# Sixteen-element attention chain: bias or mask and the extremum of each head in one VectorE instruction

## The reference

```python
sim = jnp.einsum('bhnd,bhmd->bhnm', q, k)
sim = (sim + rel_pos_bias(rel_emb, n, m)) * SCALE
attn = jax.nn.softmax(sim, axis=-1)
```

## Time and profile before

| | |
|---|---|
| median of 3 runs | 1412.81 us (1411.97 to 1413.31) |
| the profiled execution | 1414.21 us |
| its span, first to last instruction | 1411.0 us |
| instructions | 25836 |
| TensorE busy (matmuls) | 1261.4 us |
| VectorE busy | 959.5 us |
| ScalarE busy | 783.4 us |
| GpSimd busy | 339.1 us |
| mean granted clock of TensorE | 0.956 |

### The profile page before, as it was taken

How to read it: one execution, slowest core, us unless ns; L and a number is a source line. 1 busy time by engine, 2 the same in 40 slices (tenths; PEclk the granted TensorE clock), 3 DMA queues, 4 the chain that set the end, 5 groups by cost and what they waited for, 6 DMA issues and landing times.

```text
span 1411.0 us, 25836 instructions
## 1 busy us (share of the span) xinstructions
PE 1261.4 (89%) x9426; PEld 996.6 (71%) x9426; DVE 959.5 (68%) x1877; ACT 783.4 (56%) x2690; POOL 339.1 (24%) x766
## 2 busy tenths in 40 slices
PE   3567889999999999999999999999999999988755
PEld 2345667877787887877787778788787778766633
DVE  2355466969687877868696968777786869583522
ACT  1124364857565666757475756566675847464411
POOL 0101313231322232232323132223223232302020
PEclk9779999999999999999999999999999999999755
DMA  6901010100001010101000000101010100000000
GB/s 200 331 1 41 1 42 1 34 16 19 29 0 48 0 48 0 45 4 45 4 25 23 15 33 0 48 0 48 0 45 4 45 4 11 27 5 4 4 4 4
DMA packets 28586, 44.38 MB, mean 31 GB/s; under 512 B 4710, under 2 KB 20614, under 8 KB 28044
## 3 DMA queue, kind: packets, MB, share of 16 engines
q1 hardware_dynamic: 26252, 31.41, 7.0%
q0 software_dynamic: 2304, 12.58, 2.5%
HBM read 37.65 MB, written 6.34 MB: 31 GB/s over the span
## 4 chain that ended last, share of the span: by engine, by line
PE 64%; DVE 21%; ACT 11%; issue 2%; DMA 1%; POOL 1%; SPq 0%; POOLq 0%; DVEq 0%; ACTq 0%
PE psum L487 43%; PE psum L481 7%; ACT A L790 5%; ACT sa_p L790 4%; DVE small_ L1003 4%; PE psum L642 3%; PE psum L535 3%; PE psum L694 2%; PE psum L706 2%; PE psum L661 2%; DVE A L997 2%; DVE sa_p L1011 1%; DVE sa_p L997 1%; PE psum L551 1%; DVE A L1088 1%
## 5 line engine op out<-in xcount | busy, mean ns | idle before, releaser
L1279 POOL TENSOR_SCALAR small_<-small_ 128x1 f32<-128x1 f32 x112 | 37.1, 331 | 865.3 <-ACT A L908 382.5
L790 ACT ACTIVATE A<-A,small_ 128x128 f32<-128x128 f32 x384 | 148.6, 393 | 86.0 <-DVE small_ L1004 86.0
L481 PE MATMUL psum<-cst,A 128*128 128x128 f32 x672 | 108.3, 288 | 64.4 <-DVE A L1011 27.0
L783 ACT ACTIVATE A<-psum 128x1024 f32<-128x1024 f32 (+2 forms) x112 | 77.1, 688 | 156.9 <-PE psum L481 109.1
L481 PEld LDWEIGHTS psum<-cst,A 128*128 128x128 f32 x672 | 80.3, 147 | 101.4 <-DVE A L1011 40.5
L1168 DVE SCALAR_TENSOR_TENSOR A<-psum,half_cw,A 128x127 f32<-128x127 f32 (+2 forms) x288 | 75.2, 343 | 41.1 <-ACT A L894 41.1
L790 ACT ACTIVATE sa_p<-sa_p,small_ 128x128 f32<-128x128 f32 x256 | 99.1, 397 | 4.4 <-DVE small_ L1004 4.4
L790 ACT ACTIVATE ca_p<-ca_p,small_ 128x128 f32<-128x128 f32 x256 | 98.7, 391 | 4.8 <-DVE small_ L1004 4.8
L1010 DVE RECIPROCAL small_<-small_ 128x8 f32<-128x8 f32 x112 | 22.3, 199 | 91.1 <-ACT A L790 81.5
L997 DVE TENSOR_TENSOR A<-psum,cst 128x1024 f32<-128x1024 f32 x32 | 39.2, 1225 | 56.9 <-PE psum L535 56.9
L790 ACT ACTIVATION_READ_ACCUMULATOR A<-A,small_ 128x1 f32 x384 | 73.8, 192 | 0.0
(11 more groups left out here) (217 smaller groups left out, 3213.6 us busy)
## 6 DMA issues: line engine op xcount, KB each, us to landing
inT<-in_tokT SPq DMA_DIRECT2D x16, 256.0 KB, 2.9
kv_rows<-A SPq DMA_DIRECT2D x16, 256.0 KB
ctx_in<-in_ctx SPq DMA_DIRECT2D x16, 128.0 KB, 2.1
A<-bias_rows SPq DMA_DIRECT2D x1, 2048.0 KB, 9.3
Wsakv<-in_wsa_kv SPq DMA_DIRECT2D x1, 2048.0 KB, 12.7
Wcakv<-in_wca_kv SPq DMA_DIRECT2D x1, 2048.0 KB, 14.0
ctx_end<-in_tokT SPq DMA_DIRECT2D x16, 128.0 KB, 2.2
out<-x_out SPq DMA_DIRECT2D x16, 128.0 KB, 1.7
```

The costliest lines, as they stand in the source:

```text
L481: mm = pe.transpose(out[:, c * P:(c + 1) * P], src[:, c * P:(c + 1) * P], ident)
L783: return act.activation(out, in_, ACT.Copy)
L790: ins = act.activation(p[:, h * T:(h + 1) * T], p[:, h * T:(h + 1) * T], ACT.Exp, bias=sm(part, "nm", w * HU + h, w * HU + h + 1), accum_o ...
L1279: then(pool.tensor_scalar(t, src, scale, eps, ALU.mult, ALU.add))
```

## The change

All softmaxes work on negated scores. The scaling of the queries (l0, sa, ca, c3), the bias table, the window mask and the padding mask change their sign. `softmax_max` becomes `softmax_low`: for each head one VectorE instruction adds the bias or mask to 128 columns of scores, writes the sum to SBUF and writes the minimum of the head to its column of `nm`. That minimum of the negated scores is the negated maximum which the exponential needs as its bias, so the separate maximum and negation are gone, and the exponential takes the scale -1. One semaphore per layer, `lows`, is raised after the fourth and after the eighth head. ScalarE's exponentials wait for it half a unit at a time. TensorE's second group of scores in sa and ca waits for the eighth head of the first unit, where it waited for the add. The VectorE engine no longer waits for itself inside the step; one semaphore increment (`held`) stands ahead of the eight instructions. In the diff below the four lines in which the engines receive the new helper are left out.

```diff
@@ -23,6 +23,7 @@
 NEG = -1.0e9
+TOP = 3.0e38
 LOG_A_CAP = 80.0
@@ -72,7 +73,7 @@
     put("upto", (p <= j) * 1.0)
-    put("window", np.where((j >= p - 64) & (j < p + 65), 0.0, NEG))
+    put("window", np.where((j >= p - 64) & (j < p + 65), 0.0, -NEG))
     put("quad", (p // HD0 % 4 == np.arange(4)) * 1.0)
@@ -161,8 +162,7 @@

-NAMES += [f"{L}_{step}" for L in ("l0", "sa", "ca", "c3") for step in ("scores", "negmax", "exp", "probs", "PT", "PTsb")]
-NAMES += ["sa_added", "ca_added"]
+NAMES += [f"{L}_{step}" for L in ("l0", "sa", "ca", "c3") for step in ("scores", "lows", "exp", "probs", "PT", "PTsb")]

@@ -290,7 +290,7 @@

-        _soft = [("mx", 2 * HU), ("nm", 2 * HU), ("sm", 2 * HU), ("rc", 2 * HU)]
+        _soft = [("nm", 2 * HU), ("sm", 2 * HU), ("rc", 2 * HU)]
         _norm = [("bn", 6), ("mv", 2), ("r", 1), ("r1", 1), ("ssq", 1), ("ssq1", 1), ("t1", 2)]
@@ -376,7 +376,11 @@

-            return need, free, need_unit
+            def need_lows(t, L, w, half):
+
+                eng.wait_ge(sem[f"{L}_lows"], t.value(2, half + 1) if L == "c3" else t.value(4, 2 * w + half + 1))
+
+            return need, free, need_unit, need_lows

@@ -633,7 +637,7 @@
                         if w == 1:
-                            need_unit(t, f"{L}_added", 0)
+                            need_lows(t, L, 0, 1)
                         else:
@@ -785,9 +789,10 @@
                 part = PART[L]
-                need_unit(t, f"{L}_negmax", w)
                 for h in range(HU):
-                    ins = act.activation(p[:, h * T:(h + 1) * T], p[:, h * T:(h + 1) * T], ACT.Exp,
+                    if h % (HU // 2) == 0:
+                        need_lows(t, L, w, h // (HU // 2))
+                    ins = act.activation(p[:, h * T:(h + 1) * T], p[:, h * T:(h + 1) * T], ACT.Exp, scale=-1.0,
                                          bias=sm(part, "nm", w * HU + h, w * HU + h + 1),
@@ -973,7 +978,7 @@
             then(dve.tensor_copy(keep[:], pad_at))
-            dve.tensor_scalar(pad_add[:], keep[:], NEG, None, ALU.mult)
+            dve.tensor_scalar(pad_add[:], keep[:], -NEG, None, ALU.mult)
             then(dve.tensor_scalar(keep[:], keep[:], -1.0, 1.0, ALU.mult, ALU.add))
@@ -981,7 +986,7 @@
                 dve.wait_ge(sem["bias_ps"], 1)
-                dve.tensor_scalar(rows_at, Pd[0:2 * H2, 0:2 * T - 1], HD2 ** -0.5, None, ALU.mult).then_inc(sem["bias_sb"], 1)
+                dve.tensor_scalar(rows_at, Pd[0:2 * H2, 0:2 * T - 1], -HD2 ** -0.5, None, ALU.mult).then_inc(sem["bias_sb"], 1)

@@ -990,18 +995,21 @@

-            def softmax_max(t, L, w, p, scores, extra):
-
-                mx, nm = (sm(PART[L], name, w * HU, (w + 1) * HU) for name in ("mx", "nm"))
+            def held():
+
+                dve.sem_inc(sem["dve_chain"], 1)
+                steps[0] += 1
+
+            def softmax_low(t, L, w, p, scores, extra):
+
                 need_unit(t, f"{L}_scores", w)
-                ins = dve.tensor_tensor(heads(p), heads(scores), extra, ALU.add)
-                if L in LAYER:
-                    ins.then_inc(sem[f"{L}_added"], 1)
-                    need_unit(t, f"{L}_added", w)
-                else:
-                    then(ins)
-                then(dve.tensor_reduce(mx, heads(p), AX.X, ALU.max))
-                dve.tensor_scalar(nm, mx, -1.0, None, ALU.mult).then_inc(sem[f"{L}_negmax"], 1)
+                held()
+                for h in range(HU):
+                    at = slice(h * T, (h + 1) * T)
+                    ins = dve.tensor_tensor_reduce(p[:, at], scores[:, at], extra(h), 1.0, TOP, ALU.add, ALU.min,
+                                                   sm(PART[L], "nm", w * HU + h, w * HU + h + 1))
+                    if h % (HU // 2) == HU // 2 - 1:
+                        ins.then_inc(sem[f"{L}_lows"], 1)

@@ -1037,7 +1045,7 @@
                     ins = dve.tensor_scalar(q0o[:, c * T:(c + 1) * T], Pa[:, c * T:(c + 1) * T], pc("bq", c),
-                                            HD0 ** -0.5, ALU.add, ALU.mult)
+                                            -HD0 ** -0.5, ALU.add, ALU.mult)
                 ins.then_inc(sem["q0_sb"], 1)
@@ -1122,7 +1130,7 @@
                         at = slice(w * BANK, (w + 1) * BANK)
-                        dve.tensor_scalar(Q2[L][:, at], X[:, at], HD2 ** -0.5, None, ALU.mult).then_inc(sem[f"{L}_q_sb"], 1)
+                        dve.tensor_scalar(Q2[L][:, at], X[:, at], -HD2 ** -0.5, None, ALU.mult).then_inc(sem[f"{L}_q_sb"], 1)

@@ -1135,7 +1143,7 @@
                 return {f"{L}_hat": [hats], f"{L}_q": [queries],
-                        **{f"{L}_s{w}": [lambda t, w=w: softmax_max(t, L, w, (PA2, PB2)[w][L][:], X, heads(bias[:, LAYER[L], w]))]
+                        **{f"{L}_s{w}": [lambda t, w=w: softmax_low(t, L, w, (PA2, PB2)[w][L][:], X, lambda h: bias[:, LAYER[L], w, h * T:(h + 1) * T])]
                            for w in range(2)},
@@ -1213,7 +1221,7 @@
                 need(t, "c3_q")
-                dve.tensor_scalar(q3, Pd[:, 0:D], float(np.float32(1.0 / np.sqrt(HD3))), None,
+                dve.tensor_scalar(q3, Pd[:, 0:D], -float(np.float32(1.0 / np.sqrt(HD3))), None,
                                   ALU.mult).then_inc(sem["c3_q_sb"], 1)
@@ -1224,7 +1232,7 @@
                 "inputs": [inputs], "kv0": [project0],
-                **{f"l0_s{w}": [lambda t, w=w: softmax_max(t, "l0", w, probs0, P_1, spread(C("window"), HU))] for w in range(2)},
+                **{f"l0_s{w}": [lambda t, w=w: softmax_low(t, "l0", w, probs0, P_1, lambda h: C("window"))] for w in range(2)},
                 **{f"l0_p{w}": [lambda t, w=w: softmax_norm(t, "l0", w, probs0)] for w in range(2)},
@@ -1232,7 +1240,7 @@
                 "m_xh": [m_mix], "m_heads": [m_gated], "m_out": [result_m], "kv3": [keys_values3], "hat3": [normed3],
-                "q3": [query3], "c3_s": [lambda t: softmax_max(t, "c3", 0, probs3, P_4, spread(pad_add[:], HU))],
+                "q3": [query3], "c3_s": [lambda t: softmax_low(t, "c3", 0, probs3, P_4, lambda h: pad_add[:])],
                 "c3_p": [lambda t: softmax_norm(t, "c3", 0, probs3)], "c3_out": [result3],
```

More of the change, by code:

```diff
@@ L475, in _ @@
             pe.sem_inc(sem["c3_kv"], 1)
-            need, free, need_unit = need_by(pe)
+            need, free, need_unit, need_lows = need_by(pe)
             def turn(out, src, n):
@@ L779, in _ @@
             act.wait_ge(sem["prep_done"], 2)
-            need, free, need_unit = need_by(act)
+            need, free, need_unit, need_lows = need_by(act)
             def copy(out, in_):
@@ L940, in _ @@
             steps = [0]
-            need, free, need_unit = need_by(dve)
+            need, free, need_unit, need_lows = need_by(dve)
             def step(ins):
@@ L1251, in _ @@
             steps = [0]
-            need_names, free, need_unit = need_by(pool)
+            need_names, free, need_unit, need_lows = need_by(pool)
             def restart():
```

## The result

The changed kernel takes 1391.42 us (median of 4 runs, 1385.49 to 1395.54) against 1412.39 for the kernel before beside it: a ratio of 0.985, 95% interval 0.981 to 0.989, so 21 us faster. The forecast was 1397 with 1390 to 1422. Two further timings in the experiments agree: 0.985 (0.983 to 0.988) and 0.984 (0.982 to 0.987). The profiled execution took 1390.1 with a span of 1388.2; before it was 1414.21 and 1411.0. The two are not equally typical: 1390.1 is in the middle of the changed kernel's 15 timings, while 1414.21 is 3.1 above the median of the 42 timings of the kernel before (1411.1; two of them are slower). Differences between these two traces, the opening's above all, hold for the pair and are larger than those of the medians.

The account below looks back on a forecast made before the run. TensorE was taken to bound the loop, chains of waits the opening and end. Loop 5.2, opening 5.6 and end 5.8 make 16.6 us off the median 1412.81: 1396.2, named 1397, range 1390 to 1422.

Parts of the forecast that it names:

- The number: Whole kernel: 16.6 us saved from the median 1412.81 gives 1396.2, named as 1397.
- What bounds the kernel: TensorE is busy 75.06 of 76.52 us per loop turn, only 1.46 winnable; chains of waits decide opening and end.
- The price of the new instruction: VectorE, per head: 0.20 pass plus 0.09 read, x = 0.29 us; a unit takes 2.35 against 2.59.
- the tiny VectorE row: A tiny VectorE operation occupying 0.08 us, the neighbour from which the accumulator read was priced at 0.09.
- Earlier exponentials: ScalarE starts after four heads, 1.21 us after the unit's start against 2.72, so 1.5 sooner.
- bare units: Softmax units in opening and end with add, exponentials and product all on the chain; each wins 1.5 us.
- The wait that is added: TensorE's second score group waits for all eight instructions, 2.35 us against 1.22; in the loop hidden by 0.45.
- Inside the loop: Per turn 0.27 before the second sa probabilities' turn and 0.13 of small pieces: 0.40 x 13 = 5.2 us.
- Opening: 0 to 200 us: three units at 1.5, one at 0.7, VectorE time of two 0.4: 5.6 us won.
- nothing takes this back: Opening: its gain stays, as the weights have landed and POOL's folding at 141 starts when its input comes.
- End: From 1192 us: two c3_s units 3.0, steps around 1264 to 1275 1.8, the rest 0.7 and 0.27: 5.8 us.
- The rival of a VectorE bound: Loop: past x = 0.325 four units outgrow VectorE's 0.15 slack; 1423 at 0.36, 1445 at 0.40; chance 0.24.

Follow-up runs that it names:

- full_wait: The changed kernel, but ScalarE's exponentials of a unit wait for all eight heads: 1398.05 us, ratio 0.9915; timed again 1395.77 us, ratio 0.9891.
- rows_first_before: The kernel before, with the second element's inputs and the store of rows issued ahead of the late weights: 1416.76 us, ratio 1.0041.
- rows_alone_before: The kernel before, second element's inputs and first row store ahead of the late weights, which SyncE holds until the first gather lands: 1408.07 us, ratio 0.998.
- fused_plus_plain: The changed kernel, with four plain adds of 128 columns ahead of each four fused instructions: 1483.0 us, ratio 1.0521 to the kernel before.
- halves_old_ops: The kernel before, its add, maximum and negation done in halves of four heads, exponentials starting behind each half: 1433.65 us, ratio 1.0158.
- eight_adds: The kernel before, its one add of 1024 columns made as eight of 128, all else as it was: 1447.36 us, ratio 1.0254.

## Why the prediction was right, step by step

- **The number**: 15.8 us were forecast from the median and 21.0 measured. The first median, 1391.42, lies 1.4 inside the range, and the third, 1388.93, outside it. The mechanisms of loop and end held; the opening's gain came in good part for reasons that the forecast did not have, and that part is luck.
- **What bounds the kernel**: right. The loop gave little per turn, opening and end gave two thirds of the pair's 22.8.
- **The price of the new instruction**: the step with the largest error. The forecast priced a head at x = 0.29, the pass at 0.20 and the read at 0.09. Measured: 0.211, of which a plain pass is 0.197. The lower bound of 0.20 (the read costs nothing) was nearly the truth; the tiny VectorE row that I took as a model for the read was the wrong neighbour, because the read is hidden beside the next head's pass. A unit takes 1.69, not 2.35. The Trainium skill's table in "VectorE: DVE Perf Modes" ("The TRN2 errata") gave an estimate of 2.55 a unit; the trace disagrees, 1.69. The Trainium skill's rule there ("Two Vector instructions with no wait between them") that such an operation is two instructions agrees with the trace, which has 896 read records; that the second one costs the 58 cycles I had put into that estimate from the table's other column does not.
- **Earlier exponentials**: 1.5 sooner forecast; 0.97 instead of 2.72 after the unit's start, so 1.75 sooner. The bare units' waits shrank by 1.59 (7.57 to 5.98, 7.50 to 5.91), 1.61 and 1.60. The 0.16 between goes with the added semaphore increment: the end's chain has 0.19 from the product's end (1372.93) to the first fused instruction, with L1000 in it, where it was 0.02 (1394.19 to 1394.21). I had put 0.03; no run takes the increment out alone. Full_wait splits the 1.59: 0.84 is the early start, 0.75 the shorter unit and what it loses to the increment.
- **The wait that is added**: free in the loop, as predicted (no idle of TensorE before ca_s1). In the last element it shows: 1.04 before ca_s1 (1288.73), where 0.34 stood for the add, 0.7 that I had not counted. TensorE's next wait gives it back: 1.50 where 2.95 stood, so both together are 0.75 shorter.
- **Inside the loop**: 0.40 a turn forecast, 0.57 or 0.58 measured. The 0.27 before the sa probabilities went, as said, but not because of the half-unit start: full_wait has the same turn. The shorter unit alone does it. Comparing the two turns place by place, the changed one is up to 0.9 ahead at the turn of the c3 probabilities, and 0.3 of that is given back at the near-key chain ([0.54] to [0.86]): a chain that starts from TensorE's own query product, and that does not get shorter. That was predicted to stay; it grew by what reached it early.
- **Opening**: 5.6 forecast, 8.2 measured, and yet the step "nothing takes this back" was wrong, and so was its reason, "the weights have landed by then": SyncE still issues weights until 56.3. The first element's lead of 6.8 us went down to 0.3 at a store and its gather, and with it the 3.2 of the two bare units that the forecast counted on (3.0); the rest of that lead was clock. What came behind it: 1.6 of wait in the third bare unit and 0.4 in the next small waits; 1.7 because the eight products behind that unit ran at the full clock (5.40 at 103.98, 3.70 at 101.81); 2.5 where POOL folds Wmi and Wmo, shown below; and 1.4 from there to the loop's entry, 0.8 of it from the third element's l0 (forecast 0.7); the remaining 0.3 are small pieces. So two errors of opposite sign stand in this term: 3.0 of the forecast never reached the second element, and 4.2 came from TensorE's clock level, which the forecast did not contain. The 1.7 is not shown to belong to the change: the eight products took 3.70 in rows_first_before too, behind the same old wait of 2.72, and 5.40 in rows_alone_before.
- **End**: 5.8 forecast; 7.3 less the thirteenth turn's 0.6 is 6.7. By unit: the two bare c3_s waits of 3.85 and 7.50 became 2.26 and 5.91 (3.2, forecast 3.0); the three waits of 0.53, 1.20 and 0.86 became none, 0.55 and 0.33 (1.7, forecast 1.8). Of the three units with VectorE alone on the chain (forecast 0.24 each) sa_s0 gave 0.53 (TensorE's wait of 1.29 became 0.76) and the first ca unit the 0.75 above; for the third no such wait stands out. Some 0.5 is left; products of the end run at the lower clock in either kernel, not at the same places, which I did not separate.
- **The rival of a VectorE bound** did not come true, since x stayed far under 0.34. Its place is shown: units of 3.03 cost 23 and 37 us, and TensorE waits where the rival said. The slope is about 4.8 a turn for each us of unit (4.51 less the mean 2.1 of the two others, over 0.5), where I had 4; carried back from there it reaches the turn before at a unit of about 2.6 (3.03 less 2.1 / 4.8), near the 2.63 of the forecast (8 x 0.325 and the 0.03), an estimate that no run stands at. The forecast would have missed badly had the read cost what ScalarE's does (0.40 a pair).

The place of the 2.5 us, TensorE's timeline of the kernel before and of the changed one around the turn that waits for POOL's folding (POOL L1320, L1328; 7.08 and about 3.6 for its two parts in both):

```profile
153.96 0.69 PE L481 MATMUL psum<-cst,sa_p 128*128 128x128 f32 x2 [5.21 <-DVE sa_p L1019]
154.44 6.14 PE L487 MATMUL psum<-Wcakv,ca_p 128*128 128x512 f32 x8
```

```profile
142.75 5.01 PE L491 MATMUL psum<-ca_p,Wcakv 128*128 128x128 f32 x32
...
149.90 0.44 PE L485 MATMUL psum<-cst,sa_p 128*128 128x128 f32 x2 [1.08 <-DVE sa_p L1027]
150.18 3.60 PE L491 MATMUL psum<-Wcakv,ca_p 128*128 128x512 f32 x8
```

The turn is 4.06 earlier in the changed kernel, as the chain through VectorE and POOL that it waits for. Its shorter idle time is no gain: the products ahead of it ran slower (5.01 for 32, 3.74 before). But behind it the eight products take 3.60 instead of 6.14. The granted clock is 1.00 and then 0.66 in the kernel before (10 us from 140 and from 150 on), and 0.73 and then 1.00 in the changed one: the low stretch lies ahead of the wait in the one, where the wait hides it, and behind it in the other. In the thirteen profiled executions the four that idled 2.4 or more at this turn (the kernel before, its two reorderings and fused_plus_plain) took 6.14, 4.87, 4.96 and 4.80 for these eight, and the nine that idled about 1.0 took 3.60. Among the nine are halves_old_ops and eight_adds, with the old instructions and dearer units, so the 2.5 is not the price of the old softmax either. Whether the long idle time lowers the clock, or a low stretch that comes earlier merely shortens the idle time, no run separates.

Not settled: why TensorE's clock level in the opening differs between executions of one kernel (full_wait), and how much of the change's median rests on it. No experiment held the opening's clock fixed, and there is one trace of the unaltered kernel before, a slow one.

## What to carry to other kernels

Price a fused instruction by its start-to-start step in a run of its own kind, and give both bounds for its second record: here the read was free and the new unit cost a third less than the three instructions it replaced, although it has sixteen records for three. Starting the consumer at half a unit pays only where the unit is bare (0.84 each here); where the engine is 98% busy the shorter unit is the gain. And when a prologue gets faster, look at what it now arrives beside: a store or gather that found free DMA queues may meet the weight loads, and moving it ahead of them helped here only when the loads also waited until the gather had landed. Before dividing a gain of some 20 us between stretches of two traces, see how far executions of one kernel differ there: here by 6 us.

## What the runs showed of the hardware that was not expected

- A VectorE accumulator read (82 ns) starts together with the next instruction and adds no step: fused with read 0.211 a head, plain add 0.197.
- An indirect gather that takes 4.88 with the weight loads held takes 10.31 with them beside it; a store of 256 KB takes 3.10 with them held and 6.96 beside them. Issued behind them at any time from 57.85 to 62.32 it landed between 64.4 and 65.7.
- Two executions of the same kernel (full_wait) differed by 6 us at the loop's entry; the same four products take 1.13 in one and 2.08 in the other, TensorE's two clock levels.
- Behind an idle time of 5.21 eight products took 6.14, where they take 3.60 behind 1.08; all thirteen traces sort this way, the cause stays open.
